# A four-layer graph network on one core: the first layer without its table of relation products

## The reference, cut to what matters

```python
def rgcn_conv(x, edge_index, edge_type, W, W_root, b):
    src, dst = (edge_index[0], edge_index[1])
    seg = dst * N_REL + edge_type                      # N_REL = 16
    summed = jax.ops.segment_sum(x[src], seg, num_segments=N_NODES * N_REL)
    cnt = jax.ops.segment_sum(jnp.ones((src.shape[0],), x.dtype), seg, num_segments=N_NODES * N_REL)
    agg = (summed / jnp.maximum(cnt, 1.0)[:, None]).reshape(N_NODES, N_REL, x.shape[1])
    return jnp.einsum('nrd,rdh->nh', agg, W) + x @ W_root + b

h = jax.nn.relu(rgcn_conv(x, edge_index, edge_type, W1, root1, b1))
x = layernorm(x + rgcn_conv(h, edge_index, edge_type, W2, root2, b2))
```

## Time and profile before

| | us |
|---|---|
| median of 3 runs | 7771.3 (7764.43, 7771.30, 7775.73) |
| profiled execution, its own time | 7765.49 |
| its span | 7763.7 |
| mean granted clock of PE | 0.635 |
| PE, PEld, DVE busy | 4088.5, 3348.1, 2131.0 |
| ACT, POOL busy | 2024.1, 4912.0 |

### The profile page before, as it was taken

How to read it: one execution, slowest core, us unless ns; L and a number is a source line. 1 busy time by engine, 2 the same in 40 slices (tenths; PEclk the granted TensorE clock), 3 DMA queues, 4 the chain that set the end, 5 groups by cost and what they waited for, 6 DMA issues and landing times.

```text
span 7763.7 us, 97535 instructions
## 1 busy us (share of the span) xinstructions
PE 4088.5 (53%) x18001; PEld 3348.1 (43%) x18002; DVE 2131.0 (27%) x7521; ACT 2024.1 (26%) x5750; POOL 4912.0 (63%) x5278
## 2 busy tenths in 40 slices
PE   5756776693333365666666844333344444444443
PEld 3346666543333344555554433333333333344333
DVE  6743333332222235666653300000200000100001
ACT  1100000020000013444432243333333333333333
POOL 0057777617777737777750077777577777677776
PEclk9955555695655666666655766555565566666556
DMA  4412222161111113333320321112211111211112
GB/s 159 175 38 57 58 58 57 49 270 52 52 51 52 52 29 88 83 85 83 85 63 0 133 54 52 51 52 52 54 52 51 52 52 52 60 52 52 51 52 55
DMA packets 282560, 529.06 MB, mean 68 GB/s; under 512 B 120570, under 2 KB 165710, under 8 KB 269534
## 3 DMA queue, kind: packets, MB, share of 16 engines
q0 software_dynamic: 159744, 330.88, 16.8%
q1 hardware_dynamic: 117934, 193.34, 7.1%
q10 hardware_dynamic: 4656, 2.79, 0.1%
HBM read 377.76 MB, written 148.89 MB: 68 GB/s over the span
## 4 chain that ended last, share of the span: by engine, by line
POOL 47%; issue 27%; PE 15%; DVE 4%; DMA 3%; ACT 1%; DVEq 1%; POOLq 1%; SPq 0%; ACTq 0%
POOL GB L634 44%; PE PS L976 3%; PE PS L964 3%; PE PS L1076 2%; POOL H L634 2%; DMA GB<-table,IDX 2%; PE PS L1183 2%; PE PS L1027 1%; PE PS L1050 1%; DVE TOUT L1380 1%; DMA table<-TOUT 1%; PE PS L1044 1%; DVEq L459 1%; DVE TOUT L1626 0%; POOL H L681 0%
## 5 line engine op out<-in xcount | busy, mean ns | idle before, releaser
L634 POOL DMA_INDIRECT GB<-table,IDX x4160 | 3945.8, 949 | 1482.3 <-issue 1352.4
L976 PE MATMUL PS<-OH,GB 128*128 128x128 f32 x8320 | 1953.0, 428 | 2889.9 <-DMA GB<-table,IDX 2868.9
L976 PEld LDWEIGHTS PS<-OH,GB 128*128 128x128 f32 x8320 | 1802.0, 328 | 3041.6 <-issue 2663.4
L1400 DVE TENSOR_TENSOR ACC<-ACC,PS 128x128 f32 x666 | 190.0, 285 | 4336.7 <-PE PS L976 4332.7
L740 ACT COPY IDX<-idx 128x8 int32 x520 | 101.7, 196 | 2725.1 <-PE PS L976 2706.4
L729 ACT ACTIVATE OH<-iota_f,local 128x128 f32<-128x128 f32 x2496 | 761.8, 387 | 0.0
L628 POOL COPY STG<-X 128x128 f32 x150 | 48.5, 328 | 865.7 <-DVE X L1436 431.5
L634 POOL DMA_INDIRECT GB<-table_gat,IDX x416 | 421.2, 1012 | 127.6 <-issue 122.5
L634 POOL DMA_INDIRECT H<-table_gat,IDX x416 | 420.8, 1012 | 126.8 <-issue 125.6
L1183 PE MATMUL PS<-TOUT,OH 128*128 128x144 f32 x1664 | 427.3, 449 | 0.9 <-DVE TOUT L1626 0.9
L1183 PEld LDWEIGHTS PS<-TOUT,OH 128*128 128x128 f32 x1664 | 394.9, 330 | 2.5 <-issue 1.0
(11 more groups left out here) (271 smaller groups left out, 4117.6 us busy)
## 6 DMA issues: line engine op xcount, KB each, us to landing
table<-TOUT SPq DMA_DIRECT2D x100, 1024.0 KB, 3.9
GB<-table,IDX POOLq DMA_INDIRECT x4160, 2.5
TOUT<-local_row SPq DMA_DIRECT2D x104, 256.0 KB
table<-TOUT SPq DMA_DIRECT2D x50, 512.0 KB, 2.6
H<-etype_row SPq DMA_DIRECT2D x105, 64.0 KB
GB<-table_gat,IDX POOLq DMA_INDIRECT x416
H<-table_gat,IDX POOLq DMA_INDIRECT x416
table_gat<-TOUT SPq DMA_DIRECT2D x10, 340.0 KB, 2.7
```

The costliest lines, as they stand in the source:

```text
L634: pool.indirect_dma_start(out=out[:, j, :], out_offset=None, in_=r.table.dram[:, :], in_offset=bass.IndirectOffsetOnAxis(ap=idx[:, j:j + 1 ...
L976: return nc.tensor.matmul(PS[:, bank, 0:P], GB[:, b, j * r.width:j * r.width + P], oh(b, j), **at)
```

## The change

The first layer does its sums before its products. The inner sum is linear, so instead of gathering products, a round gathers raw rows (x in round one, relu of the first result in round two), sums them per near node and relation, and multiplies by the 16 matrices once per batch:

- `table16`, both its makings, and the look-up of weights through `aux` on PE are gone. The relations' broadcasts on SP go too.
- The preparation computes `key16` = 16 x (target - first target of the tile) + relation for each edge, `place` (which window column each of the 8 x 16 near nodes of a batch belongs to), and clamps the ends of tiles to the last node. X is copied by ACT instead of DVE; root1 + b1 are put into `sums` before the round by PE and ACT.
- The counting runs alone. The counts are transposed (nodes on partitions, 50 x 16 columns), inverted there and stored to DRAM as `one_over`, 400 KB.
- In a round, for each batch: POOL gathers 8 x 128 rows of 512 bytes into one of four buffers (ROWS) instead of two; SP (round one only) loads for each tile the 256 inverse counts from its first target on, broadcast over 128 partitions (WINDOWS); DVE makes 8 one-hots of 128 x 256 weighted by them (round two: by `wcol`); PE sums 8 tiles into 4 PSUM banks of 512 columns; ACT copies these, reordered to relation-major, to NEARBY; PE multiplies 16 blocks of 128 columns by 16 weight blocks into one bank; ACT copies it to MADE; PE places the 128 near nodes in the window by a one-hot PLACED; DVE adds to `sums`. The products of a batch come one batch behind its sums, its placing two behind.
- A tile whose targets span 16 nodes or more takes a slow path (`wide`), 8 sums per tile, all steps waiting on each other; the flag is per batch.
- Between the rounds DVE forms relu into H, PE transposes 49 blocks of `sums`, ACT applies relu, SP stores them to `table1`, and root2, b2 and X are put into `sums`. Behind round two only the layer norm is left.

```diff
-        table16 = nc.dram_tensor("table16", [NODES_P * R16, P], FP32, kind="Internal").ap()
+        one_over = nc.dram_tensor("one_over", [NODES_P, R16], FP32, kind="Internal").ap()
...
+        HOT = [OH[:, :, :].rearrange("p b n -> p (b n)"), H[:, 0:2 * G * P]]
+        ROWS = [GB[:, 0, 0:G * P], GB[:, 1, 0:G * P], H[:, 2 * G * P:3 * G * P], H[:, 3 * G * P:4 * G * P]]
+        WINDOWS = [H[:, 4 * G * P:6 * G * P], WR[:, 0:2 * G * P]]
...
@@ SP @@
+            sp.dma_start(one_over.rearrange("(k p) r -> p k r", p=P), COUNTS.rearrange("p (k r) -> p k r", r=R16)).then_inc(over_out, 16)
...
+            def windows(k, b, first):
+                if not first:
+                    sp.wait_ge(near_hot, k - 1)
+                bases = meta_of(sp, k, 4 + G, G)
+                for j in range(G):
+                    sp.dma_start(WINDOWS[b][:, j * RCOLS:(j + 1) * RCOLS],
+                                 one_over.rearrange("n r -> (n r)")[bass.ds(bases[j] * R16, RCOLS)].unsqueeze(0)
+                                 .to_broadcast([P, RCOLS])).then_inc(win_in[b], 16)
...
@@ POOL @@
-            stage_table(t_l0a, [])
+            def gather_near(r):
+                with pool.Fori(0, BATCHES // FOUR) as i:
+                    for c in range(FOUR):
+                        k = FOUR * i + c
+                        pool.wait_ge(near_idx, k + (r.first + 1))
+                        pool.sem_inc(near_passed, 1)
+                        for j in range(G):
+                            pool.indirect_dma_start(
+                                out=ROWS[c][:, j * P:(j + 1) * P], out_offset=None, in_=r.dram[:, :],
+                                in_offset=bass.IndirectOffsetOnAxis(ap=IDX[:, c, j:j + 1], axis=0),
+                            ).then_inc(near_in[c], 16)
-            gather(r_l0a)
-            stage_table(t_l0b, [sums])
-            gather(r_l0b)
+            gather_near(near_a)
+            pool.wait_ge(h_stored, 16 * GROUPS)
+            pool.wait_ge(root_ps, GROUPS)
+            gather_near(near_b)
...
@@ ACT, per batch (step) @@
+                        for n in range(r.UNITS):
+                            act.wait_ge(near_ps, K * r.UNITS + (n + 1))
+                            of, to = PS[:, n, :], NEARBY[b].rearrange("p (r s) -> p r s", r=R16)[:, :, n * 32:(n + 1) * 32]
+                            act.copy(to.rearrange("p r (j d) -> p r j d", j=2), of.rearrange("p (j d r) -> p r j d", j=2, d=NEAR))\
+                                .then_inc(near_sb, 1)
+                    if now < BATCHES - FOUR:
+                        stage(k + FOUR, c)
+                    if 1 <= now <= BATCHES:
+                        act.wait_ge(made_ps, K)
...
+                        act.copy(MADE[1 - b][:, :], PS[:, 4, 0:P]).then_inc(made_sb, 1)
...
@@ PE, per batch (step) @@
+                        with pe.Else():
+                            wide(k, b)
+                        pe.wait_ge(near_in[c], i * (16 * G) + 16 * G * (r.first // FOUR + 1))
+                        pe.wait_ge(near_hot, K + 1)
+                        for n in range(r.UNITS):
+                            if now + here >= 1:
+                                pe.wait_ge(near_sb, (K - 1) * r.UNITS + (n + 1))
+                            for j in (2 * n, 2 * n + 1):
+                                ins = nc.tensor.matmul(PS[:, n, j % 2 * RCOLS:(j % 2 + 1) * RCOLS], ROWS[c][:, j * P:(j + 1) * P],
+                                                       HOT[b][:, j * RCOLS:(j + 1) * RCOLS], start=True, stop=True)
+                            ins.then_inc(near_ps, 1)
+                    if 2 <= now <= BATCHES + 1:
...
+                        nc.tensor.matmul(PS[:, 5, 0:P], MADE[b][:, :], PLACED[b][:, :], start=True, stop=True).then_inc(placed, 1)
+                    if 1 <= now <= BATCHES:
+                        pe.wait_ge(near_sb, K * r.UNITS)
...
+                        for t in range(R16):
+                            ins = nc.tensor.matmul(PS[:, 4, 0:P], NEARBY[1 - b][:, t * P:(t + 1) * P],
+                                                   r.weights[:, t * P:(t + 1) * P], start=t == 0, stop=t == R16 - 1)
+                        ins.then_inc(made_ps, 1)
...
@@ DVE @@
-            dve.reciprocal(aux[0:R16, :], aux[0:R16, :]).then_inc(rt_ready, 1)
+            dve.reciprocal(COUNTS, COUNTS).then_inc(degree, 1)
...
+                def hot(k, b, at_half):
...
+                        dve.wait_ge(near_ps, (K - 1) * r.UNITS)
+                    if r.looks:
+                        dve.wait_ge(win_in[b], at_half * (16 * G))
+                    for j in range(G):
+                        to, key = HOT[b][:, j * RCOLS:(j + 1) * RCOLS], key16[:, bass.ds(k * G + j, 1)]
+                        if r.looks:
+                            ins = dve.scalar_tensor_tensor(to, iota_w[:, :], key, WINDOWS[b][:, j * RCOLS:(j + 1) * RCOLS],
+                                                           ALU.is_equal, ALU.mult, accum_out=wstage[:, b, j:j + 1])
+                        else:
+                            ins = dve.tensor_scalar(to, iota_w[:, :], key, wcol[:, bass.ds(k * G + j, 1)], ALU.is_equal, ALU.mult)
+                    ins.then_inc(near_hot, 1)
...
+                        dve.tensor_tensor(dst, dst, PS[:, 5, 0:P], ALU.add).then_inc(added, 1)
...
@@ PE, between the rounds @@
+                for n, q in enumerate(blocks_of(g)):
+                    ins = nc.tensor.transpose(PS[:, g % 4, n * P:(n + 1) * P], sums[:, q * P:(q + 1) * P], ident[:, :])
+                ins.then_inc(h_ps, 1)
...
+                nc.tensor.matmul(PS[:, 4 + g % 4, 0:here.stop - here.start], mat("L0_gnn_root2"), H[:, here],
+                                 start=True, stop=True).then_inc(root_ps, 1)
```

More of the change, by code:

```diff
@@ new lines, in _ @@
+            stage, step = near_round(near_a)
+            act.wait_ge(turn_sb, 1)
+            for c in range(FOUR):
+                stage(c, c)
+            for n in range(N_XG):
+                act.wait_ge(turn_ps, N_COLS + n + 1)
+                w = min(512, XBLOCKS * P - 512 * n)
+                act.copy(X[:, 512 * n:512 * n + w], PS[:, n % 8, 0:w]).then_inc(turn_a, 1)
+            for c in range(CHUNKS):
+                act.wait_ge(ground_ps, c + 1)
+                act.activation(sums[:, c * CHUNK:(c + 1) * CHUNK], PS[:, c % 4, 0:CHUNK], ACT.Identity, bias=vec("L0_gnn_b1"))\
+                    .then_inc(ground_sb, 1)
@@ L1113, in _ @@
+            pe.wait_ge(root_sb, GROUPS)
+            pe.wait_ge(h_made, GROUPS)
+            pe.wait_ge(w2_in, 16)
+            near_round(near_b)
+            pe.wait_ge(added, 2 * BATCHES)
+            node_products(n_l0b, [], layer_norm("sums", 0, None, 1, 1), [])
             multiply_table(t_gat)
```

715 lines of the change are left out of this document (455 added, 260 removed).

## The result

The changed kernel takes 7360.8 us (7355.3 to 7361.9, 4 runs) against 7767.9 of the kernel before in the same comparison: a ratio of 0.9475, 95% interval 0.9458 to 0.9491, 407 us less. Predicted were 7381. The profiled execution took 7361.67 us, its span is 7359.8, and 7375 had been worked out for it. The sum came out within 14 us, but it did so with errors of 38 and 16 us on one side and of 31, 21, 8 and 7 on the other, and the 31 have a cause that the prediction had in hand and used in one place only. That these errors cancel to 14 is luck.

The account below looks back on a forecast made before the run. POOL's indirect gathers were taken to bound both rounds; gains of 177.6 + 10.6 + 182.1 - 4.8 + 24.4 = 390 us gave 7375 for the profiled execution and 7381 us for the median, range 7320 to 7570.

Parts of the forecast that it names:

- Clock and PE against POOL: Both new rounds: PE needs 7.3 us a batch at full clock and keeps POOL's pace above mean clock 0.72; chance 0.72.
- Rivals A and B: Both rounds: A, clock stays low, 8280 us, chance 0.05; B, clock near 0.63 or hand-over gaps, 7650 us, chance 0.11.
- Round one and two: The two relation rounds, paced by POOL's gathers: round one 1066.6 to 1056 us, round two 1066.2 to 1071.
- The start-up of 8 us: Start of round one: the fifth batch's gathers wait until the first sums have left their buffer, 8 us.
- the DVE delay: Both rounds: DVE's one-hots hold up POOL's gathers they meet, taken as 0.24 us a batch.
- The tail: End of each round, behind the last gather: landing, sums, products, copies, placing and add, 11 us.
- Up to the first sum: Everything ahead of round one's first sum: 472.6 to 295 us, with counting 203 us at 1.95 a batch.
- the chain of 37: Between counting and first sum: transposes, reciprocal, store of inverse counts, first windows and one-hots, 37 us (28 to 55).
- Between the rounds: The step from round one to round two: second table goes, transposes, stores and root2 passes come, 207.1 to 25 us.
- Layer norm: First layer's norm behind round two: root2, bias and residual leave the pairs, 80.4 to 56 us (52 to 70).
- Everything behind is left as it was: All stages after the first layer's norm: no change, gain 0.
- Rival D: Both rounds: batches take the slow path because a tile spans 16 nodes, some 120 us a slow batch; chance 0.03.

Follow-up runs that it names:

- fillers: The changed kernel with two more 128x400 products, which nobody reads, beginning each pair of the first layer's layer norm: 7344.9 us, ratio 0.9451.

## Why the prediction came out right

- **Clock and PE against POOL: right.** The forecast took PE's 7.3 us a batch at a clock that follows a lagging PE up. It needed 0.72 and found 0.93. Doubling the products showed the mechanism (1.00), thinning them out showed that it had room. Rivals A and B rested on the clock of the earlier trace rows; a PE that is busy for 80% of a round got another clock than one that waits 6.27 us ahead of each burst. The busy share alone doesn't order the rows: the old round one was busy for 68% at a clock of 0.57, the thinned rounds for 62% at 0.82 and 0.84. (The passes are counted here as the rows count them, 16 for the 8 tiles of a batch, two a tile; the four a tile in the description of the old round is not what the rows show.)
- **Round one and two: right in kind, 21 and 7 us too long.** The start-up of 8 us was exact (332.7 to 340.74). The batch was 10.09 and 10.06 instead of 10.37 and 10.19, because the old pace of 10.13 held seven gaps of 3.1 us a round that the new rounds don't have, and because the DVE delay was sized at 0.24 us a batch where no more than 0.04 was measured. The formula behind it, d x d / 2.5, fitted L1626 but doesn't carry over: the new one-hots last 0.48 us (L1722), for which it gives 0.7 us a batch; why they delay so little is open. For the 0.06 us that round two has above 10.13 the prediction gives no row. The tail was mis-sized the other way, 17.7 us instead of 11; a part of that is PE's clock, which was 0.50 in the first 1.3 us behind PE's wait of 2.9 us for the last gather: the sums there take 5.1 us instead of 3.6.
- **Up to the first sum: mis-sized by 38.** "With the register loads and the loop I take 1.95" failed: 2.37 a batch, at the dear end of the bounds, 44 us more. The 1.79 had been read from the last batches of the old counting, which stand outside the loop, as written-out code. Rows from inside the old loop would not have helped: there the flags are loaded ahead of a copy of the table, and the adds of two batches follow each other by 1.53 us (376.32 and 377.85). Preparation (50.0 instead of 55) and the chain of 37 (35.8) were right.
- **Between the rounds: right,** 17.1 against 25, cheaper than the lower bound of 18; the transposes and root products ran at clock 1.00.
- **Layer norm: mis-sized by 16.** "What stays of a pair" was taken from rows at a clock of 0.78. The work taken out was PE's, and with it went the clock. What was worked out for the rounds, that PE's load makes its clock, was not carried to this stage. The clock is a part of the miss only: with it back at 0.84 the stage took 63.1 us, fillers included, still 7 more than the 56.
- **"Everything behind is left as it was": wrong by 31.** The step failed by its reach: the prediction saw that the old round ended with 8 single adds "which the new clamping spares", yet counted that in round two alone. The flag is computed once and read by every round. In the kernel before, the clamp alone is worth 77 us by the medians and 55 by the stages; so something like 14 to 19% of the whole gain of 407 doesn't come from the new way of summing at all.
- **Rival D:** the slow path never ran, as argued; its price was nearer 200 us a batch than 120, measured on the slower chip.

## What to carry to other kernels

Before costing a change, list who else reads each flag, bound or index table that it computes anew: here one line with a minimum reached seven rounds. Take the price of a loop's batch from rows of a loop with the same body and nothing else in it, since the same instructions written out cost a quarter less. And when work leaves PE in a stage with short bursts, cost what stays at the clock that the stage will then have; a stage can get shorter by giving PE more to do.

## What was not expected of the hardware

**A chip on which the same loops take longer.** In the last comparison every kernel took longer, the kernel before 9469 us instead of 7768, and the change was worth 204 us instead of 407. Single instructions last as long as elsewhere (the gathers 944 ns, the 128x512 copies 592), and the counting takes the same 246.9 us. The changed kernel's counting, round one, round two and a later sum round there:

```profile
49.70:296.60 246.90, 105.29 (x832) 76.74 (x832) 174.23 (x307) 0.00 (x0) 41.95 (x32) 0.50 0.05 12
332.20:1782.30 1450.10, 979.60 (x5201) 846.69 (x5201) 397.65 (x1961) 264.04 (x620) 762.78 (x800) 0.82 0.48 112
1799.40:3215.30 1415.90, 946.36 (x5200) 817.58 (x5200) 337.02 (x1040) 268.40 (x621) 791.89 (x832) 0.80 0.15 39
5357.90:6604.80 1246.90, 420.01 (x1799) 381.57 (x1797) 51.15 (x164) 392.60 (x1093) 784.02 (x831) 0.61 0.17 44
```

The new rounds are 40 and 33% longer, the sum round 19%. PE's timeline in round two shows where:

```profile
1903.83 2.32 PE L1296 MATMUL PS<-OH,H 128*128 128x256 f32 x10
1906.30 0.38 PE L1296 MATMUL PS<-OH,H 128*128 128x256 f32 x1 [0.15 <-issue]
1907.73 0.38 PE L1296 MATMUL PS<-OH,H 128*128 128x256 f32 x1 [1.05 <-issue]
1909.87 0.38 PE L1296 MATMUL PS<-OH,H 128*128 128x256 f32 x1 [1.76 <-issue]
1911.98 0.58 PE L1296 MATMUL PS<-OH,H 128*128 128x256 f32 x1 [1.73 <-issue]
```

In the middle of 16 passes that wait for no semaphore PE starts one instruction every 2 us, and passes go from 0.38 to 0.58 us as the clock drops behind it. In round two this idle time sums to 250.6 us ahead of the sums (L1296); on the ordinary chip it is nil. The kernel before with the clamp, in its profile on this chip, has the two old rounds:

```profile
464.80:1888.90 1424.10, 753.55 (x3309) 671.49 (x3310) 388.25 (x1959) 20.11 (x102) 783.19 (x816) 0.57 0.17 42
2101.50:3342.90 1241.40, 386.04 (x1664) 358.84 (x1664) 251.90 (x928) 21.61 (x104) 791.09 (x832) 0.58 0.17 44
```

Both hold two batches in a turn of their loop, yet the first, with 32 passes of PE a batch, loses some 360 us and the second, with 16, some 180. The new rounds, with 50 passes a batch and four batches in a turn, lose 415 and 352; the sum round, with 17, loses 197; the counting, with 8, nothing. So the loss grows roughly with PE's passes a batch, and the number of batches in a turn doesn't explain it: the old round one loses as much as the new round two. Round two's heavier loss, 352 against some 180, is most of why the change is worth 204 us there and not 407. That it is the supply of instructions is my reading of idle time with no wait behind it; no run here measures the fetch itself, and why this chip is slower is open.

**A gather that comes 3.1 us after the last.** It happens every 112 gathers in the rounds with two row buffers, 13 us a round, and not in those with four; the loop's length is ruled out, the cause is open.
